# A graph transformer, linear attention and a graph-routed expert layer in one kernel: a reload cut in fifths, a shorter early scatter, two moves, and one-hots transposed on TensorE

## The chip, the cores and the metric

One Trainium2 chip, one of its cores. The metric is device time in microseconds for one execution. Three executions of the kernel before took 7434.32, 7432.77 and 7426.59 us: median 7432.77.

## The reference, cut to what matters

```python
xn = layernorm(x)                                   # x: 6250 nodes x 256
x = x + gnn(xn, edges) + mix(xn)                    # edges: 200,000 pairs src, dst
x = x + ffn(layernorm(x), edges)

def gnn(x, edges):                                  # 6250 x 256 -> 6250 x 256, inner width 128, 8 heads
    e = x @ W_P + b + pos
    for (q, k, v, s, t) in two layers:              # per edge: exp(clip(q[row] . k[col])) per head
        att = exp(clip((e[rows] @ q) * (e[cols] @ k) summed per head, -10, 10))
        e = layernorm(segment_sum(att * (e[cols] @ v), rows) / segment_sum(att, rows) + e) * s + t
    return e @ inv_w + inv_b

def mix(x):                                         # linear attention over all nodes, 8 heads
    q, k, v = elu(rms(x) @ w_q) + 1, elu(rms(x) @ w_k) + 1, rms(x) @ w_v
    h = x + (q @ (k.T @ v)) / (q @ sum(k)) @ w_out + b_out
    return h + rms(h)

def ffn(x, edges):                                  # 4 heads x 4 experts, 131,072 of ffn's own edges
    h = x @ W_gat
    e = leaky_relu(a_src[src] + a_dst[dst]); top = segment_max(e, dst)
    w = exp(e - top[dst])                           # softmax per target node
    agg = segment_sum(w * h[src], dst) / segment_sum(w, dst)
    gate = softmax of the two best of layernorm(agg) over experts
    return sum over 4 experts of gate[e] * (gelu(x @ W1[e] + b1[e]) @ W2[e] + b2[e])
```

## The kernel before, in words

Nodes lie in 50 tiles of 125. Edges are first sorted by the tile of their target; a sorted edge tile holds 128 edges that all point into one node tile. Sums over edges are then matrix products with one-hot matrices: edge by node-in-tile (`hot`), or its transpose (`hot_t`).

The kernel is a row of blocks. Each block ends in a barrier that all engines reach, so a block lasts as long as its longest chain, its DMA waits included. The blocks, in order:

- **place** sorts the graph's 200,000 edges and scatters packed records into a table in HBM. **unpack** (line 531) reads the table back (`lists`), unpacks indices and local node numbers, and stores the local numbers to HBM as rows (`loc_rows`). Its SyncE queue also issues the load of x (5 chunks of 10 tiles, each in two pieces, 1120 and 130 KB) through `also`, ahead of that store, and waits for the store at its end.
- **enter** (line 1771): layer norm, the projection and the first q, k, v, a node tile at a time. TensorE's order for step n is `times_w(n)`, `turn(n+1)`, `project(n-1)`. ScalarE's is `copy_kv(n-1)` (two copies: q, and k with v), then `copy_turned(n+1)`. `times_w(n+1)` waits for `copy_turned(n+1)`. The turned tiles share one PSUM buffer.
- **att1** and **att2** (`attend`, line 705): 417 groups of 4 edge tiles. GpSimd issues 4 indirect gathers of k and v for each group into 4 slots, and takes a slot again when VectorE has weighted it (`weighted`). SyncE loads the group's local numbers, broadcast to all partitions, 4 groups ahead. A second body of work runs in the same steps: in att1 the keys of the linear attention and the sort of the second edge list, in att2 the rest of the linear attention (`Mix`, line 1514), a tile every 8 steps. The second sort keeps its 27 blocks of packed records in SBUF: the first 14 (`SCATTER_FIRST`) in `placed.early`, which lies in the memory of x (the arena), the others in `placed.late`. Mix needs x again: `Mix.sync` issues all 5 chunks ahead of `load_local`'s first load.
- **between** (line 2030): the norm of layer 1, then q, k, v of layer 2, in chunks of 10 tiles. GpSimd clears the sums of each chunk and scatters its share of the 14 early record blocks, 3 indirect DMAs a block, and waits for each block before the next.
- **leave** (line 2128): the norm of layer 2, the output projection, the second layer norm. GpSimd scatters the 13 late blocks. A second unpack follows.
- **max** (`neighbour_max`): maximum over neighbours, beside the expert layer.
- **sum** (`neighbour_sum`, line 2455): 141 steps of 8 edge tiles. `near_hot` compares the broadcast local numbers with the lane number and gives `hot_t`; `fetch` multiplies it by node data; `gather_info`, `sums`, `leaky`, `less`, `exps`, `weigh` make the weights; `high`, `rest_of`, `middle`, `low` split them into three bf16 parts; `one_hot` makes `hot` on VectorE; `add_up` multiplies; `add_sum(0..3)` adds into `acc3`, each waiting for the one before. What an engine does in step n, and in what order, is the list given to `steps`: a pair (lag, piece) runs the piece for k = n + lag. VectorE: info(n), add 0, leaky, add 1, near_hot(n+2), add 2, one_hot(n-2), add 3. GpSimd: sums(n), less(n-1), weigh(n-2), rest_of(n-3), low(n-4). TensorE: add_up(n-5), fetch(n+1).
- **gates** and **answer**: routing weights, weighted sum of the experts' results, output.

Of the kernel before, what the change touches and what calls it, by code (L numbers as in the profile page):

```python
# [8 lines left out]
ALU = mybir.AluOpType  # L9
# [515 lines left out]
def unpack(nc, st, c, g, also=None, loc_type=BF16, sign=1.0):  # L525
# [5 lines left out]
    with ExitStack() as us:  # L531
# [9 lines left out]
        @block.sync  # L541
        def _(sp):
            sp.dma_start(lists[:], g.table.rearrange("(q p l) -> p q l", p=LANES, l=LANES)).then_inc(m["lists_in"], 16)
            if also is not None:
                also(sp)
            sp.wait_ge(m["row_ready"], 1)
            sp.dma_start(g.loc_rows.rearrange("(q p l) -> p q l", p=LANES, l=LANES), row16[:])\
                .then_inc(m["rows_out"], 16)
            sp.wait_ge(m["rows_out"], 16)

# [438 lines left out]

SCATTER_FIRST = 14  # L990

# [520 lines left out]
class Mix:  # L1512
# [39 lines left out]
    def sync(self, sp):  # L1552
        m, ins = self.m, self.ins
        sp.dma_start(self.wq[:], ins["L0_mix_w_qkv"][:, 0:GIN].rearrange("(c p) n -> p c n", p=LANES))\
            .then_inc(m["w_in"], 16)
        sp.dma_start(self.wo[:], ins["L0_mix_w_out"].rearrange("(c p) n -> p c n", p=LANES)).then_inc(m["w_in"], 16)
        sp.dma_start(self.w1[:], ins["L0_mix_w_norm1"].rearrange("(c p) -> p c", p=LANES),
                     allow_slow_non_contiguous=True).then_inc(m["w_in"], 16)
        sp.dma_start(self.b[:], ins["L0_mix_b_out"].rearrange("(a n) -> a n", a=1)).then_inc(m["w_in"], 16)
        load_row(sp, self.w2[:], ins["L0_mix_w_norm2"], m["w_in"])  # L1560
        load_row(sp, self.shift[:], ins["L0_gnn_inv_b"], m["w_in"])
        load_x(sp, ins, self.X, self.x_in)

    def load(self, sp, n):
        pass

# [193 lines left out]

def load_x(sp, ins, X, x_in):

    source = ins["x"].rearrange(TILE_ROWS, p=NODE_TILE)
    for i in range(X.shape[1] // CHUNK):
        a = slice(i * CHUNK, (i + 1) * CHUNK)
        deal(sp, X[:, a], source[:, a], x_in[i])


def enter(nc, c, ins, x_in, X, E, qs, kv, acc, mean, rstd, mean_rstd, mix_rstd, ratio, x_turned):
# [4 lines left out]
    with ExitStack() as st:  # L1774
# [166 lines left out]
        def _(act):  # L1941
# [24 lines left out]
            for n in range(-early, tiles + 1):  # L1966
                if closed(n + early):
                    a = chunk_of(n + early)
                    act.wait_ge(m["var_ready"], (n + early) // CHUNK + 1)
                    act.activation(rstd[:, a], var[:, a], ACT.Sqrt, bias=c.eps5[0:NODE_TILE, 0:1])\  # L1970
                        .then_inc(m["std_ready"], 1)
                if closed(n + early - 1):
                    a = chunk_of(n + early - 1)
                    act.wait_ge(m["ms_ready"], (n + early - 1) // CHUNK + 1)
                    act.activation(ratio[:, a], ratio[:, a], ACT.Sqrt, bias=c.eps6[0:NODE_TILE, :])\
                        .then_inc(m["root_ready"], 1)
                if 0 <= n - 1 < tiles:
                    copy_kv(n - 1, (n - 1) % 2)
                if 0 <= n + 1 < tiles:
                    copy_turned(n + 1, (n + 1) % 2)  # L1980
            act.wait_ge(m["q_copied"], tiles)
# [47 lines left out]

def between(nc, c, ins, acc, E, qs, kv, placed):  # L2030

    tiles = E.shape[1]
    chunks = tiles // CHUNK
    with ExitStack() as st:
# [17 lines left out]
        def _(sp):  # L2052
            normal.sync(sp)
            for i, n in enumerate("qkv"):
                sp.dma_start(w[:, i * D:(i + 1) * D], ins[f"L0_gnn_{n}2"]).then_inc(m["w_in"], 16)
            rows = kv[0:NODES].rearrange("(t p) d -> t p d", p=NODE_TILE)
            for t in range(tiles):
# [398 lines left out]
def neighbour_sum(nc, c, g, src_sb, node_info, gacc, ans):  # L2456

    pairs = WIDE // PAIR
    with ExitStack() as st:
# [3 lines left out]
        def psum(n):  # L2463
            return [st.enter_context(nc.psum_tensor(f"gs_{n}{h}", [LANES, 512], F32)) for h in range(2)]

        node_no = sb("node_no", [LANES, WIDE, NODE_TILE], BF16)
        hot = sb("hot", [LANES, 4, WIDE, NODE_TILE], BF16)
        local = sb("local", [LANES, 4, WIDE * LANES], BF16)
        hot_t = sb("hot_t", [NODE_TILE, 2, WIDE * LANES], BF16)
        info = sb("info", [LANES, 4, WIDE, 2 * FH])  # L2470
# [6 lines left out]
        ps_n, ps_sum = psum("ps_n"), psum("ps_sum")  # L2477
        m = sem_set(nc, st, "gs", ["tiles_in", "cleared", "one_hots", "near_hots", "fetched", "info", "sums", "leaky",
                                   "less", "exps", "weighted", "high", "rest", "middle", "split", "summed", "added",
# [55 lines left out]
        def _(pe):  # L2535
# [7 lines left out]
            def fetch(k, r, j):  # L2543
                pe.wait_ge(m["near_hots"], k + 1)
                wait(pe, m["info"], k - 1)
                for p in range(pairs):
                    t = numbers.of(k * pairs + p)
                    for e in range(PAIR * p, PAIR * (p + 1)):
                        ins = pe.matmul(ps_n[j % 2][:, e * SPLIT * 2 * FH:(e + 1) * SPLIT * 2 * FH],
                                        hot_t[:, j % 2, e * LANES:(e + 1) * LANES],  # L2550
                                        at(node_info, t).rearrange("p n f -> p (n f)"), start=True, stop=True)
                ins.then_inc(m["fetched"], 1)

            def add_up(k, r, j):
# [9 lines left out]
                ins.then_inc(m["summed"], 1)  # L2564
            steps(pe, [(1, load_tiles), (-5, add_up), (1, fetch)])

        @block.scalar
        def _(act):
# [10 lines left out]
            def middle(k, r, j):  # L2579
                act.wait_ge(m["rest"], k + 1)  # L2580
                act.copy(parts[:, k % 4, :, 1, :], rest[:, k % 4]).then_inc(m["middle"], 1)
            steps(act, [(-3, high), (-4, middle), (-1, exps)])

        @block.vector
        def _(dve):
            chain = Chain(dve, m["chain"])
            dve.memset(acc3[:], 0.0)
            chain(dve.tensor_copy(node_no[:], c.node_no[:, 0:1, :].broadcast_to([LANES, WIDE, NODE_TILE])))
            dve.wait_ge(m["tiles_in"], 16)
# [6 lines left out]

            def one_hot(k, r, j):
                wait(dve, m["summed"], (k - 4) + 1)
                dve.tensor_tensor(hot[:, k % 4], node_no[:], g.loc[:, bass.ds(k * WIDE, WIDE)].unsqueeze(2)
                                  .broadcast_to([LANES, WIDE, NODE_TILE]), ALU.is_equal).then_inc(m["one_hots"], 1)  # L2600

            def near_hot(k, r, j):
                dve.wait_ge(m["local_in"][j], (r + 1) * 16)
                wait(dve, m["fetched"], k - 1)
                dve.tensor_scalar(hot_t[:, j % 2, :], local[0:NODE_TILE, j], c.lane_no[0:NODE_TILE, :], None, ALU.is_equal)\
                    .then_inc(m["near_hots"], 1)
# [11 lines left out]
            def add_sum(p):  # L2618
                def add(k, r, j):
# [7 lines left out]
            steps(dve, [(0, gather_info), (-6, add_sum(0)), (-1, leaky), (-6, add_sum(1)), (2, near_hot), (-6, add_sum(2)),  # L2627
                        (-2, one_hot), (-6, add_sum(3)), (-6, load_tiles)])
            dve.wait_ge(m["added"], pairs * total)
# [280 lines left out]
def program(nc, ins, out):  # L2910
    with ExitStack() as ctx:
# [27 lines left out]
        with ExitStack() as gs:  # L2939
# [3 lines left out]
            x_again = gs.enter_context(semaphores(nc, [f"x_again{i}" for i in range(tiles // CHUNK)]))  # L2943
            unpack(nc, gs, c, gnn, lambda sp: load_x(sp, ins, X, x_in), F32, -1.0)
            acc = sb(gs, "acc", [NODE_TILE, tiles, SUMS])
# [5 lines left out]
            with ExitStack() as qs_stack:  # L2951
# [5 lines left out]
                kept.close()  # L2957
                between(nc, c, ins, acc, E, qs, kv, placed)
                attend(nc, c, "att2", gnn, qs, kv, acc, lambda st: Mix(nc, c, st=st, **mix))
# [38 lines left out]
```

## Time and profile before

| | us |
|---|---|
| executions | 7434.32, 7432.77, 7426.59 |
| profiled execution | 7436.28 |
| its span, first to last instruction | 7434.6 |

| engine | busy us | share |
|---|---|---|
| TensorE matmul | 5178.4 | 70% |
| VectorE | 5381.4 | 72% |
| ScalarE | 2567.8 | 35% |
| GpSimd | 5053.4 | 68% |

Stages in the trace, by start, in us from the span's start: unpack 539, enter 575, att1 742, between 2964, att2 3074, leave 5222, second unpack 5393, max 5410, sum 6866, gates and answer 7294. Shares are averages over stages with different limits, so each stage is read by itself. In a row, PE is TensorE's matmul and PEld its weight load, DVE VectorE, ACT ScalarE, POOL GpSimd, SP SyncE; a q behind the name is the engine's queue of DMA issues; L and a number is a line of the kernel, which may be a helper's.

### The profile page before, as it was taken

What the parts mean: (1) busy time and instruction counts of PE and PEld (TensorE: products, weight loads), DVE (VectorE), ACT (ScalarE), POOL (GpSimd) and SP (SyncE); (2) the same over time, 40 slices, a digit from 0 to 9 for tenths busy, and PEclk for the clock granted to TensorE, in tenths of its full rate; (3) what the DMA queues carried; (4) which work ended last, traced back from release to release, by engine and by line L of the source; (5) the groups of instructions that cost most, each with busy time, mean ns of one, the idle gap of its engine ahead of it and who ended that gap; (6) DMA issues with size and microseconds to landing.
All of it is one profiled execution on the core that took longest, in us unless ns stands there. A gap on an engine that the chain in (4) does not pass through costs nothing. (4 is left out here: it accounts for less than half of the span.)

```text
span 7434.6 us, 108730 instructions
## 1 busy us (share of the span) xinstructions
PE 5178.4 (70%) x27327; PEld 4108.7 (55%) x27327; DVE 5381.4 (72%) x15227; ACT 2567.8 (35%) x8277; POOL 5053.4 (68%) x5420
## 2 busy tenths in 40 slices
PE   5985676767777776466666666666679999998440
PEld 3654455556666665256656555555546666665330
DVE  8983676667777776467777777776767777777997
ACT  0002444443344433344444444444322222222330
POOL 1430677777777776577777777777267777776991
PEclk7558788887878777777777888888668888887555
DMA  1013544444444443444444444444323323232437
GB/s 27 4 26 92 138 138 137 139 130 122 124 121 124 124 124 110 112 132 131 131 131 131 131 131 131 131 131 129 106 52 63 60 59 63 59 63 60 121 92 185
DMA packets 510444, 783.73 MB, mean 105 GB/s; under 512 B 121690, under 2 KB 370617, under 8 KB 509837
## 3 DMA queue, kind: packets, MB, share of 16 engines
q0 software_dynamic: 202656, 454.22, 23.2%
q1 hardware_dynamic: 299233, 311.35, 15.5%
q10 hardware_dynamic: 7948, 11.21, 0.6%
q8 instruction: 241, 3.95, 0.2%
q14 instruction: 366, 3.00, 0.1%
HBM read 705.00 MB, written 71.36 MB: 104 GB/s over the span
## 5 line engine op out<-in xcount | busy, mean ns | idle before, releaser
L695 POOL DMA_INDIRECT att_kv_e<-kv,gnn_idx x3336 | 3278.6, 983 | 1238.2 <-issue 984.7
L772 PE MATMUL att_ps_sum<-att_vals,att_hot 128*125 128x136 f32 x6672 | 1290.7, 350 | 1358.1 <-DVE att_vals L826 1356.8
L772 PEld LDWEIGHTS att_ps_sum<-att_vals,att_hot 128*125 128x125 f32 x6672 | 1095.9, 238 | 1588.7 <-DVE att_vals L826 1572.4
L695 POOL DMA_INDIRECT max_rows<-rows,gat_idx x1128 | 1065.6, 945 | 469.5 <-issue 337.4
L807 DVE TENSOR_TENSOR att_prod<-att_ps_q,att_kv_e 128x512 f32<-128x512 f32 x834 | 575.9, 691 | 990.0 <-issue 401.9
L759 PE MATMUL att_ps_q<-qs,att_hot_t 125*128 x6672 | 1182.1, 336 | 104.8 <-DVE att_hot_t L814 104.8
L759 PEld LDWEIGHTS att_ps_q<-qs,att_hot_t 125*128 125x128 f32 x6672 | 1127.8, 254 | 106.1 <-issue 106.1
L790 ACT ACTIVATE att_hot<-node_no,gnn_loc 128x125 f32<-128x125 f32 x3336 | 1044.4, 384 | 22.8 <-PEq L86 22.8
L783 ACT ACTIVATE att_ps_dve<-att_clipped 128x32 f32<-128x32 f32 x834 | 167.7, 201 | 2442.0 <-DVE att_clipped L834 2441.3
L2399 DVE CUSTOM_DVE_ANT_0 max_junk<-max_far,max_ps_b 125x256 bf16<-125x256 bf16 x2256 | 793.3, 416 | 260.2 <-PE max_ps_b L2363 258.7
L842 DVE TENSOR_TENSOR acc<-acc,att_ps_sum 125x136 f32 x1668 | 485.6, 291 | 125.2 <-DVE acc L842 8.2
L820 DVE TENSOR_REDUCE att_dots<-att_prod 128x32 f32<-128x512 f32 x834 | 563.8, 676 | 0.1
L826 DVE TENSOR_TENSOR att_vals<-att_kv_e,att_ps_dve 128x512 f32<-128x512 f32 x834 | 563.6, 676 | 0.0
L795 ACT ACTIVATE att_hot<-att_hot 128x500 f32<-128x500 f32 x834 | 513.9, 616 | 17.4
L2798 PE MATMUL ex_ps_o<-ex_w,ex_hid 128*125 128x256 f32 x1600 | 518.4, 480 | 0.0
L814 DVE TENSOR_SCALAR att_hot_t<-att_local,lane_no 125x512 f32<-125x512 bf16 x834 | 416.1, 499 | 123.6 <-DMA att_local<-gnn_loc_rows 123.6
L2363 PE MATMUL max_ps_b<-max_a_t,pick_head 12*125 12x512 bf16 x1128 | 376.1, 434 | 64.7 <-ACT max_a_t L2372 52.1
L2824 ACT ACTIVATE ex_hid<-ex_ps_h,ex_b 128x250 f32<-128x250 f32 x400 | 165.6, 465 | 726.5 <-PE ex_ps_h L2809 726.4
L2809 PE MATMUL ex_ps_h<-ex_xT,ex_w 128*128 128x250 f32 x1600 | 414.2, 404 | 0.0
L2798 PEld LDWEIGHTS ex_ps_o<-ex_w,ex_hid 128*125 128x125 f32 x1600 | 356.6, 235 | 88.9 <-issue 14.2
L510 POOL DMA_INDIRECT gnn_table<-gnn_records,gnn_dest_sb x120 | 173.9, 1449 | 337.7 <-DVE gnn_records L426 300.5
L2809 PEld LDWEIGHTS ex_ps_h<-ex_xT,ex_w 128*128 128x128 f32 x1600 | 343.4, 215 | 57.8 <-issue 0.4
(450 smaller groups left out, 7501.2 us busy)
## 6 DMA issues: line engine op xcount, KB each, us to landing
att_local<-gnn_loc_rows SPq DMA_DIRECT2D x834, 128.0 KB
att_kv_e<-kv,gnn_idx POOLq DMA_INDIRECT x3336
max_local<-gat_loc_rows SPq DMA_DIRECT2D x282, 128.0 KB
gs_local<-gat_loc_rows SPq DMA_DIRECT2D x141, 256.0 KB, 3.2
outs<-ex_y SPq DMA_DIRECT2D x25, 896.0 KB
max_rows<-rows,gat_idx POOLq DMA_INDIRECT x1128
X<-in_x SPq DMA_DIRECT2D x10, 1120.0 KB
ans_late<-outs SPq DMA_DIRECT2D x11, 896.0 KB
```

What stands on the lines that cost most here:

```text
L695: pool.indirect_dma_start(rows(j, e), None, source, bass.IndirectOffsetOnAxis(ap=g.idx[:, t:t + 1], axis=0))\
L759: ins = pe.matmul(ps_q[j % 2][:, e * D:(e + 1) * D], hot_t[:, j % 2, e * LANES:(e + 1) * LANES], at(qs, t), start=True, stop=True)
L772: ins = pe.matmul(ps_sum[j % 2][0:NODE_TILE, p * 256:p * 256 + SUMS], hot[:, j, PAIR * p + e, :], vals[:, j % 2, PAIR * p + e, :], start=e ...
L790: act.activation(hot[:, j, e, :], c.node_no[:, 0, :], ACT.Abs, bias=g.loc[:, t:t + 1])\
L795: act.activation(hot[:, j], hot[:, j], ACT.Relu, scale=-1.0, bias=1.0).then_inc(m["one_hots"], 1)
L807: dve.tensor_tensor(prod[:].rearrange("p (e d) -> p e d", e=GROUP), ps_q[j % 2][:, :].rearrange("p (e d) -> p e d", e=GROUP), kv_e[:, j, : ...
L820: dve.tensor_reduce(dots_sb[:, j % 2, :], prod[:].rearrange("p (h d) -> p h d", d=HEAD), AX, ALU.add).then_inc(m["dots"], 1)
L826: dve.tensor_tensor(vals[:, j % 2, :, 0:D].rearrange("p e (h d) -> p e h d", d=HEAD), kv_e[:, j, :, D:2 * D].rearrange("p e (h d) -> p e h ...
L842: dve.tensor_tensor(a, a, ps_sum[j % 2][0:NODE_TILE, p * 256:p * 256 + SUMS], ALU.add)\
L2399: ins = dve.tensor_tensor_reduce(out=junk[:, j % 2, 2 * n + i, :], in0=far[:, j % 2, i * 256:(i + 1) * 256], in1=ps_b[n][0:NODE_TILE, i * ...
L2798: ins = pe.matmul(self.ps_o[0:NODE_TILE, 0:GIN], self.hid[:, e % 2, hc, k * NODE_TILE:(k + 1) * NODE_TILE], self.w2[:, e, hc, :], start=hc ...
L2809: ins = pe.matmul(self.ps_h[:, i * TWO:(i + 1) * TWO].rearrange("p (t n) -> p t n", t=2), self.w1[:, e, ch, a:a + LANES], self.xT[:, s % 2 ...
```

## The change

- `unpack` issues the store of `loc_rows`, and waits for it, on ScalarE instead of SyncE. It serves both graphs.
- `SCATTER_FIRST` is 8 instead of 14: 8 record blocks are scattered in between, 19 in leave.
- x is reloaded chunk by chunk: chunk 0 in between, ahead of its k and v stores; chunks 1 to 4 in att2, at steps 40, 120, 200 and 280.
- In enter, ScalarE does `copy_turned(n+1)` ahead of `copy_kv(n-1)`.
- In sum, `one_hot` and its constant are gone. `turn_hots(n-1)`: 8 transposes of `hot_t` on TensorE, behind fetch, into two new PSUM buffers. `copy_hots(n-2)`: one copy of them into `hot` on ScalarE, behind exps. `hot_t` has 4 buffers, which come free on the transposes.

```diff
@@ unpack
-            sp.wait_ge(m["row_ready"], 1)
-            sp.dma_start(g.loc_rows..., row16[:]).then_inc(m["rows_out"], 16)
-            sp.wait_ge(m["rows_out"], 16)
+        @block.scalar
+        def _(act):
+            act.wait_ge(m["row_ready"], 1)
+            act.dma_start(g.loc_rows..., row16[:]).then_inc(m["rows_out"], 16)
+            act.wait_ge(m["rows_out"], 16)
@@
-SCATTER_FIRST = 14
+SCATTER_FIRST = 8
@@ Mix
-        load_x(sp, ins, self.X, self.x_in)                       # in sync
     def load(self, sp, n):
-        pass
+        i, late = divmod(n + MIX_PACE * CHUNK // 2, MIX_PACE * CHUNK)
+        if late == 0 and 0 < i < self.tiles // CHUNK:
+            load_x(sp, self.ins, self.X, self.x_in, i, i + 1)
@@ load_x
-    for i in range(X.shape[1] // CHUNK):
+    for i in range(first, last):
@@ enter, ScalarE
+                if 0 <= n + 1 < tiles:
+                    copy_turned(n + 1, (n + 1) % 2)
                 if 0 <= n - 1 < tiles:
                     copy_kv(n - 1, (n - 1) % 2)
-                if 0 <= n + 1 < tiles:
-                    copy_turned(n + 1, (n + 1) % 2)
@@ between, SyncE, behind the loads of w
+            load_x(sp, ins, X, x_in, 0, 1)
@@ neighbour_sum
-        node_no = sb("node_no", [LANES, WIDE, NODE_TILE], BF16)
-        hot_t = sb("hot_t", [NODE_TILE, 2, WIDE * LANES], BF16)
+        hot_t = sb("hot_t", [NODE_TILE, 4, WIDE * LANES], BF16)
+        ps_hot = [... nc.psum_tensor(f"gs_ps_hot{h}", [LANES, 1024], BF16) for h in range(2)]
+            def turn_hots(k, r, j):                                # TensorE
+                wait(pe, m["one_hots"], k - 1)
+                for e in range(WIDE):
+                    ins = pe.transpose(ps_hot[j % 2][:, e * LANES:e * LANES + NODE_TILE],
+                                       hot_t[:, k % 4, e * LANES:(e + 1) * LANES], c.ident16[0:NODE_TILE, 0:NODE_TILE])
+                ins.then_inc(m["turned"], 1)
-            steps(pe, [(1, load_tiles), (-5, add_up), (1, fetch)])
+            steps(pe, [(1, load_tiles), (-5, add_up), (1, fetch), (-1, turn_hots)])
+            def copy_hots(k, r, j):                                # ScalarE
+                act.wait_ge(m["turned"], k + 1)
+                wait(act, m["summed"], (k - 4) + 1)
+                act.copy(hot[:, k % 4], ps_hot[j % 2][:]....[:, :, 0:NODE_TILE]).then_inc(m["one_hots"], 1)
-            steps(act, [(-3, high), (-4, middle), (-1, exps)])
+            steps(act, [(-3, high), (-4, middle), (-1, exps), (-2, copy_hots)])
-            def one_hot(k, r, j):                                  # VectorE
-                wait(dve, m["summed"], (k - 4) + 1)
-                dve.tensor_tensor(hot[:, k % 4], node_no[:], g.loc[...]..., ALU.is_equal).then_inc(m["one_hots"], 1)
             def near_hot(k, r, j):
-                wait(dve, m["fetched"], k - 1)
+                wait(dve, m["turned"], (k - 4) + 1)
-            steps(dve, [(0, gather_info), (-6, add_sum(0)), (-1, leaky), (-6, add_sum(1)), (2, near_hot), (-6, add_sum(2)),
-                        (-2, one_hot), (-6, add_sum(3)), (-6, load_tiles)])
+                        (-6, add_sum(3)), (-6, load_tiles)])
```

## Rows read from the trace of the kernel before

**Rows 1.** Timeline, unpack's end: start, length, engine, line, operation, [idle before, releaser].
```profile
539.87 23.62 SPq L649 DMA_DIRECT2D X<-in_x  x10
563.53 0.49 SPq L547 DMA_DIRECT2D gnn_loc_rows<-gnn_row  x1
575.20 5.76 POOL L1834 MEMSET acc<- 125x6800 f32 x1 [39.56 <-POOLq L86]
```

**Rows 2.** Timeline of one tile of enter.
```profile
729.58 0.81 PE L1929 MATMUL enter_ps_p<-enter_w,enter_ET 128*125 128x384 f32 x2
...
730.85 0.39 ACT L1957 COPY enter_xT<-enter_ps_t 128x250 f32<-128x250 f32 x1
...
731.29 0.71 PE L1921 MATMUL enter_ps_e<-enter_xT,enter_wp 128*128 128x125 f32 x4 [0.90 <-ACT enter_xT L1957]
```

**Rows 3.** Waits in enter: engine, line, releaser, us in total, times, longest.
```profile
PE enter_ps_e L1921 <- ACT enter_xT L1957: 44.2, 50, 0.9
```

**Rows 4.** Timeline of the end of enter: last stores, first issue of att1.
```profile
736.64 2.35 SPq L649 DMA_DIRECT2D kv<-enter_kv_sb  x4
...
741.92 0.23 SPq L738 DMA_DIRECT2D att_tile_of<-gnn_pair_tile  x1
```

**Rows 5.** Timeline of the end of between and the start of att2.
```profile
3035.86 19.82 SPq L649 DMA_DIRECT2D kv<-between_kv_sb  x29
...
3073.68 0.22 SPq L738 DMA_DIRECT2D att_tile_of<-gnn_pair_tile  x1
...
3076.49 37.66 SPq L649 DMA_DIRECT2D X<-in_x  x10
...
3123.46 0.88 DVE L814 TENSOR_SCALAR att_hot_t<-att_local,lane_no 125x512 f32<-125x512 bf16 x2 [84.24 <-DMA att_local<-gnn_loc_rows]
...
3130.56 0.94 POOL L695 DMA_INDIRECT att_kv_e<-kv,gnn_idx  x1 [36.45 <-DVE att_vals L826]
```

**Rows 6.** Tile `gat_table`, scatters: ns min/median/max, first to last start, form.
```profile
L1010 POOL DMA_INDIRECT gat_table<-X,placed_dest x42: 952/999/2094, 2980.9 to 3066.4; - x42
L1010 POOL DMA_INDIRECT gat_table<-placed_late,placed_dest x39: 952/958/1947, 5223.6 to 5310.5; - x39
```

**Rows 7.** Windows, sum stage: stretch, us, busy us by engine, clock, DMA share, GB/s.
```profile
6866.00:7294.00 428.00, 180.28 (x2256) 165.46 (x2256) 415.77 (x1133) 123.81 (x423) 408.71 (x705) 0.50 0.34 100
```

**Rows 8.** Timeline of VectorE in one step of sum.
```profile
7103.53 1.19 DVE L2599 TENSOR_TENSOR gs_hot<-gs_node_no,gat_loc 128x1000 bf16<-128x1000 bf16 x1
...
7106.44 1.19 DVE L2599 TENSOR_TENSOR gs_hot<-gs_node_no,gat_loc 128x1000 bf16<-128x1000 bf16 x1
...
7107.55 0.20 DVE L2623 TENSOR_TENSOR gs_acc<-gs_acc,gs_ps_sum 125x60 f32 x1
```

**Rows 9.** Timeline of VectorE in sum's last steps: one add behind another.
```profile
7284.42 0.22 DVE L2623 TENSOR_TENSOR gs_acc<-gs_acc,gs_ps_sum 125x60 f32 x1 [0.21 <-DVE gs_acc L2623]
```

**Rows 10.** Timeline of GpSimd in one step of sum.
```profile
7104.79 0.41 POOL L2508 TENSOR_TENSOR gs_vals<-src_sb,gs_vals 128x128 f32<-128x128 f32 x1
...
7106.46 1.28 POOL L2530 TENSOR_TENSOR gs_e_sb<-gs_e_sb,gs_info 128x32 f32<-128x32 f32 x1
```

**Rows 11.** Tile `gs_e_sb`, columns as in rows 6.
```profile
L2610 DVE SCALAR_TENSOR_TENSOR gs_e_sb<-gs_e_sb x141: 174/511/518, 6873.5 to 7276.4; 128x32 f32<-128x32 f32 x141
L2530 POOL TENSOR_TENSOR gs_e_sb<-gs_e_sb,gs_info x141: 244/1275/1281, 6874.1 to 7277.3; 128x32 f32<-128x32 f32 x141
```

**Rows 12.** Tile `gs_hot_t`, columns as in rows 6.
```profile
L2605 DVE TENSOR_SCALAR gs_hot_t<-gs_local,lane_no x141: 472/639/765, 6870.8 to 7268.7; 125x1024 bf16<-125x1024 bf16 x141
```

**Rows 13.** Timeline of TensorE in one step of sum.
```profile
7106.16 1.06 PE L2560 MATMUL gs_ps_sum<-gs_parts,gs_hot 128*125 128x60 bf16 x8 [1.64 <-POOL gs_parts L2520]
...
7107.04 0.39 PE L2549 MATMUL gs_ps_n<-node_info,gs_hot_t 125*128 x8
```

**Rows 14.** Timeline of TensorE in max: four transposes.
```profile
6000.35 0.39 PE L2354 MATMUL max_ps_a<-ident,max_rows 128*12 128x128 bf16 x4
```

**Rows 15.** Lines, a ScalarE copy: busy us, mean ns, idle before.
```profile
L2372 ACT COPY max_a_t<-max_ps_a 12x512 bf16<-12x512 bf16 x282 | 161.9, 574 | 371.9 <-PE max_ps_a L2354 371.9
```

More of the change, by code:

```diff
@@ L545, in _ @@
                 also(sp)
-            sp.wait_ge(m["row_ready"], 1)
-            sp.dma_start(g.loc_rows.rearrange("(q p l) -> p q l", p=LANES, l=LANES), row16[:])\
+        @block.scalar
+        def _(act):
+            act.wait_ge(m["row_ready"], 1)
+            act.dma_start(g.loc_rows.rearrange("(q p l) -> p q l", p=LANES, l=LANES), row16[:])\
                 .then_inc(m["rows_out"], 16)
-            sp.wait_ge(m["rows_out"], 16)
+            act.wait_ge(m["rows_out"], 16)
         @block.tensor
@@ L1758, with load_x @@
 CHUNK = 10
-def load_x(sp, ins, X, x_in):
+def load_x(sp, ins, X, x_in, first, last):
     source = ins["x"].rearrange(TILE_ROWS, p=NODE_TILE)
-    for i in range(X.shape[1] // CHUNK):
+    for i in range(first, last):
         a = slice(i * CHUNK, (i + 1) * CHUNK)
@@ L2027, in scalar, with between @@
             .then_inc(m["root_ready"], 1)
-def between(nc, c, ins, acc, E, qs, kv, placed):
+def between(nc, c, ins, acc, E, qs, kv, placed, X, x_in):
     tiles = E.shape[1]
@@ L2477, in neighbour_sum @@
         ps_n, ps_sum = psum("ps_n"), psum("ps_sum")
-        m = sem_set(nc, st, "gs", ["tiles_in", "cleared", "one_hots", "near_hots", "fetched", "info", "sums", "leaky",
+        ps_hot = [st.enter_context(nc.psum_tensor(f"gs_ps_hot{h}", [LANES, 1024], BF16)) for h in range(2)]
+        m = sem_set(nc, st, "gs", ["tiles_in", "cleared", "turned", "one_hots", "near_hots", "fetched", "info", "sums", "leaky",
                                    "less", "exps", "weighted", "high", "rest", "middle", "split", "summed", "added",
@@ L2549, in fetch @@
                         ins = pe.matmul(ps_n[j % 2][:, e * SPLIT * 2 * FH:(e + 1) * SPLIT * 2 * FH],
-                                        hot_t[:, j % 2, e * LANES:(e + 1) * LANES],
+                                        hot_t[:, k % 4, e * LANES:(e + 1) * LANES],
                                         at(node_info, t).rearrange("p n f -> p (n f)"), start=True, stop=True)
                 ins.then_inc(m["fetched"], 1)
+            def turn_hots(k, r, j):
[4 more added lines that the diff above has]
+                ins.then_inc(m["turned"], 1)
             def add_up(k, r, j):
@@ L2581, in middle @@
                 act.copy(parts[:, k % 4, :, 1, :], rest[:, k % 4]).then_inc(m["middle"], 1)
-            steps(act, [(-3, high), (-4, middle), (-1, exps)])
+            def copy_hots(k, r, j):
+                act.wait_ge(m["turned"], k + 1)
+                wait(act, m["summed"], (k - 4) + 1)
+                act.copy(hot[:, k % 4], ps_hot[j % 2][:].rearrange("p (e n) -> p e n", e=WIDE)[:, :, 0:NODE_TILE])\
+                    .then_inc(m["one_hots"], 1)
+            steps(act, [(-3, high), (-4, middle), (-1, exps), (-2, copy_hots)])
         @block.vector
@@ L2586, in _ @@
             chain = Chain(dve, m["chain"])
-            dve.memset(acc3[:], 0.0)
-            chain(dve.tensor_copy(node_no[:], c.node_no[:, 0:1, :].broadcast_to([LANES, WIDE, NODE_TILE])))
+            chain(dve.memset(acc3[:], 0.0))
             dve.wait_ge(m["tiles_in"], 16)
@@ L2595, in gather_info @@
                                   .rearrange("p (e n f) -> p e f n", e=WIDE, n=SPLIT), AX, ALU.add).then_inc(m["info"], 1)
-            def one_hot(k, r, j):
-                wait(dve, m["summed"], (k - 4) + 1)
-                dve.tensor_tensor(hot[:, k % 4], node_no[:], g.loc[:, bass.ds(k * WIDE, WIDE)].unsqueeze(2)
-                                  .broadcast_to([LANES, WIDE, NODE_TILE]), ALU.is_equal).then_inc(m["one_hots"], 1)
             def near_hot(k, r, j):
                 dve.wait_ge(m["local_in"][j], (r + 1) * 16)
-                wait(dve, m["fetched"], k - 1)
-                dve.tensor_scalar(hot_t[:, j % 2, :], local[0:NODE_TILE, j], c.lane_no[0:NODE_TILE, :], None, ALU.is_equal)\
+                wait(dve, m["turned"], (k - 4) + 1)
+                dve.tensor_scalar(hot_t[:, k % 4, :], local[0:NODE_TILE, j], c.lane_no[0:NODE_TILE, :], None, ALU.is_equal)\
                     .then_inc(m["near_hots"], 1)
@@ L2943, in program @@
             x_again = gs.enter_context(semaphores(nc, [f"x_again{i}" for i in range(tiles // CHUNK)]))
-            unpack(nc, gs, c, gnn, lambda sp: load_x(sp, ins, X, x_in), F32, -1.0)
+            unpack(nc, gs, c, gnn, lambda sp: load_x(sp, ins, X, x_in, 0, tiles // CHUNK), F32, -1.0)
             acc = sb(gs, "acc", [NODE_TILE, tiles, SUMS])
@@ L2957, in program @@
                 kept.close()
-                between(nc, c, ins, acc, E, qs, kv, placed)
+                between(nc, c, ins, acc, E, qs, kv, placed, X, x_again)
                 attend(nc, c, "att2", gnn, qs, kv, acc, lambda st: Mix(nc, c, st=st, **mix))
```

## The prediction, made before the change was run

> **What bounds the kernel now.** I read the windows by stage first, then the waits of each stage that the change touches, then the timeline where a wait ends last. A barrier stands between stages, so what a stage loses is lost for good.
>
> In unpack the reader is to see SyncE: its issue of x ends at 539.87 + 23.62 = 563.49, the store behind it goes out at 563.53, and enter starts only at 575.20 [rows 1]. In enter TensorE stands still for 0.90 us in each tile until the turned tile is copied [rows 2], 44.2 us over 50 tiles [rows 3]. Between ends with the scatters: the last starts at 3066.4 [rows 6], the k and v stores are issued by 3035.86 + 19.82 = 3055.68, and att2 starts at 3073.68 [rows 5]. In att2 GpSimd's gathers set the pace, but it stands for 36.45 us once, since the first local numbers land behind all of x: VectorE waits 84.24 us for them [rows 5]. In sum VectorE is busy 415.77 of 428 us and GpSimd 408.71; TensorE runs at a granted clock of 0.50, its 1.2 GHz level [rows 7]. One step takes 7106.44 - 7103.53 = 2.91 us, and `one_hot` has 7107.55 - 7106.44 = 1.11 of it [rows 8]. While it runs, GpSimd's `less` takes 1.275 us instead of 0.244 [rows 10, 11]: both engines wait for one thing.
>
> **The change part by part.** The sum goes against the profiled execution, 7436.28 us; the median of the runs is 3.5 below it.
>
> *Unpack's store.* It leaves ScalarE as soon as VectorE has the rows, and SyncE's end is then the end of the issue of x. From the end of the last issue to the first of the next block enter took 741.92 - 738.99 = 2.93 us, with landing [rows 4]; so enter can start near 563.49 + 2.9 = 566.4, 8.8 us earlier. The store is 0.46 MB beside 6.4 MB of x, whose issue may take 1.7 us longer (23.62 x 0.46 / 6.4). Enter's first weights now move while x still lands. Bounds: 0 (the store lands as late as now) to -10. I take -7, nearer to the SyncE row. The other unpack has no load of x in front: 0. The row says that the store waits behind x in its queue. The Trainium skill (DMA: Bandwidth & Descriptors, Issuing engines are not separate DMA queues) says that transfers from all issuing engines run on the same 16 DMA engines and interleave; it speaks against a gain beyond the issue. By it alone this term would be the 0.49 us of issue, by the rows it is 7.
>
> *Enter's copies.* ScalarE copies the next turned tile while `project` (0.81 us) runs: the copy takes 0.39 [rows 2], and `turn` stands ahead of `project`. So the 0.90 goes: 50 x 0.90 = 45. Queued behind the moved copy are q, k and v of the tile before; only `project` of the next step waits for them, a whole `times_w` and `turn` later. Late next is VectorE: a step of 2.0 us leaves little beside its chain of statistics every tenth tile. Bounds -20 (half is lost there or to stores that now come every 2 us) to -45. I take -40, near the row.
>
> *Between.* 42 scatters took 2980.9 to 3066.4, 2.04 us each [rows 6]. 24 fit in 49 us, and the last chunk has 6 instead of 9. Then the stores end last: 3055.68 + 2.93 = 3058.6, against 3073.68: -15. Chunk 0 of x, 1.25 MB, goes out ahead of the first store, where the queue is idle while VectorE norms its first chunk: 0; without that cover it would delay the stores by 7.5 us, a fifth of 37.66 [rows 5]. Bounds -8 to -18.
>
> *Leave* gets 18 more scatters: 39 took 86.9 us [rows 6], so 57 take 127 and end near 5351, over 40 us ahead of the next block at 5393: 0; at worst +5 by crowding the stores.
>
> *att2's start.* The local loads go out at 3076.49 instead of 37.7 us later, so the first slot comes free near 3130.56 - 37.7 = 3092.9. GpSimd has gathers to issue until 3130.56 - 36.45 = 3094.1 [rows 5]. All 36.45 go. In return four chunks run during the gathers, each with 7.5 us of queue time ahead of the local loads of four groups. A group lasts 5.15 us (417 in 2148 us), and loads run four groups, 20 us, ahead: hidden, but I leave 2.5 for it. Without the cover it is 4 x 7.5 = 30. Bounds -6 to -36.5; I take -34, near the cover.
>
> *Sum.* VectorE loses 1.11 of 2.91 us. But `add 2` and `add 3` now stand side by side, and each add waits for the one before: 0.22 + 0.21 = 0.43 us from one to the next [rows 9], where one now takes 0.20 [rows 8] with other work between: +0.23, or +0.3 with the issue. That is 2.1. GpSimd: from `weigh` at 7104.79 to `less` at 7106.46 are 1.67 us [rows 10], with an undisturbed `less` 1.9. TensorE: `add_up` and `fetch` from 7106.16 to 7107.43, 1.27 [rows 13], and 8 transposes. Max did four in 0.39 us [rows 14]; at the 1.2 GHz level eight are 0.8 to 0.9 (125 columns each): 2.1 to 2.2 at that clock, less if it rises. ScalarE: 123.81 / 141 = 0.88 a step [rows 7] and one copy of 1000 columns. No row has it; 512 columns took 0.574 [rows 15], so it lies between 0.6 and 1.12: at most 2.0. All four engines then need 1.9 to 2.2, and I take a step of 2.2, a tenth over VectorE's: 0.71 x 138 steps in the steady part = 98. Bounds: a step of 1.9 gives -139, one of 2.9 gives 0. Two waits are new. `turn_hots` waits for the copy two steps back, with `add_up` queued behind it; `add_up` waits for `copy_hots`, which ran two steps ahead. Neither is last as long as ScalarE keeps up.
>
> Sum: 7 + 40 + 15 + 34 + 98 = 194. 7436.28 - 194 - 3.5 = **7239 us**.
>
> **Rivals.** *The shared port (20%).* `less` shows that a VectorE instruction and one of GpSimd exclude each other [rows 10, 11]. `hot_t` and `leaky` stretch too, 0.472 to 0.639 and 0.174 to 0.511 [rows 11, 12]. If they exclude all of GpSimd's work, a step is 1.91 + 0.47 + 0.17 = 2.55: 0.36 x 138 = 50 instead of 98, 7287 us. Against it: GpSimd's 1.67 us were measured with both of them beside it. The Trainium skill (SBUF — State Buffer, Who interferes with whom) has such a rule: VectorE with two inputs in SBUF, or in its two-port modes, and GpSimd lock one port pair for a whole instruction. By that rule the trace agrees for `one_hot`.
>
> *x in the way of the local loads (10%).* Each chunk stops the gathers for its 7.5 us; 30 of the 36 come back: 7267. For it: they stood 36 us for that in the trace; against it: that was at a start, with no group ahead.
>
> *TensorE in series, slower (4%).* `add_up` waits for the last of GpSimd's pieces, `fetch` stands behind it, the transposes behind that. If the two steps of lag that part these are eaten up, a step is 1.9 + 1.27 + 0.86 = 4.03 us: 1.12 x 138 = +155, with the other terms, -96, and the 3.5: 7492. It decides from 2.91 + 96 / 138 = 3.6 us a step. For it: TensorE waits 1.64 us for that piece in each step [rows 13]; against: with the same lags this costs the step nothing today.
>
> *More than forecast (10%).* A step of 1.95, enter 44, between 18: 7 + 44 + 18 + 36 + 132 = 237, 7196.
>
> **How the numbers follow.** The forecast has 56%, with a range of its own of 7205 to 7275. The range 7185 to 7310 takes in the port, the queue and most of the better case. Leaving out 4% for the slow rival and 1% for terms that just cancel: faster 0.95, same 0.01, slower 0.04 (0.2%, 15 us, is what a measurement of this kernel can tell from none).
>
> **What would show it.** Enter within 3 us of unpack's last issue of x; no wait of TensorE for the turned tile and about 2.0 to 2.1 us a tile; att2 starting right behind the last k and v stores; no gap of GpSimd at att2's start, and none at steps 40, 120, 200 and 280; in sum steps of 2.2 us with `less` near 0.25 to 0.45. I am wrong if ScalarE's copy takes over 1.2 us, if TensorE's transposes hold up `fetch`, or if VectorE waits in enter.

## The result, and the profile after

The changed kernel takes 7250.86 us (median of 4, 7240.77 to 7260.62) against 7431.77 beside it: ratio 0.9757, 95% interval [0.974, 0.9774]. Forecast was 7239. The profiled execution is the slowest of the four, 7260.62. Stages are read from their first instructions. The change in means compares the traces of all runs, those of the experiments below included, that have the old or the changed code in that stage; in brackets stands how many have the changed code.

| stage | before | after | change in means | forecast |
|---|---|---|---|---|
| unpack's end | 35.8 | 30.2 | -7.1 (10 runs) | -7 |
| enter | 166.7 | 117.4 | -48.8 (9) | -40 |
| att1 | 2223.5 | 2216.5 | -1.2 (11) | 0 |
| between | 108.3 | 93.1 | -14.7 (9) | -15 |
| att2 | 2150.0 | 2128.7 | -29.5 (7) | -34 |
| leave, second unpack | 186.1 | 186.1 | +1.0 (10) | 0 |
| max | 1456.5 | 1456.7 | +0.5 (11) | 0 |
| sum | 427.9 | 348.9 | -81.7 (6) | -98 |
| gates, answer | 140.4 | 140.8 | +0.3 (11) | 0 |

The means add up to -181; the medians differ by 180.9. att1 and att2 vary by some 10 us from run to run, mostly in the sum of their gathers' own durations (1593.5 to 1602.8 us in att2), so one pair of traces can't size a few us there.

The timeline at unpack's end (start, length, engine, line, operation, [idle before]) answers to [rows 1]: x's issue ends at 569.62, and enter starts 1.1 us behind it instead of 11.7.

```profile
540.98 28.64 SPq L652 DMA_DIRECT2D X<-in_x  x10
...
551.73 0.42 ACTq L550 DMA_DIRECT2D gnn_loc_rows<-gnn_row  x1
...
570.73 5.76 POOL L1838 MEMSET acc<- 125x6800 f32 x1 [33.98 <-POOLq L86]
```

One tile of enter, as [rows 2]: the copy now runs beside `project`, and the next product follows at once. One tile takes 661.22 - 659.40 = 1.82 us.

```profile
659.40 0.81 PE L1933 MATMUL enter_ps_p<-enter_w,enter_ET 128*125 128x384 f32 x2
...
659.60 0.37 ACT L1961 COPY enter_xT<-enter_ps_t 128x250 f32<-128x250 f32 x1 [0.63 <-PE enter_ps_t L1916]
...
660.04 0.68 PE L1925 MATMUL enter_ps_e<-enter_xT,enter_wp 128*128 128x125 f32 x4
...
661.22 0.81 PE L1933 MATMUL enter_ps_p<-enter_w,enter_ET 128*125 128x384 f32 x2
```

Of the 44.2 us of waits in [rows 3] 2.3 are left:

```profile
PE enter_ps_e L1925 <- ACT enter_xT L1961: 2.3, 6, 0.5
```

Between's end, as [rows 5]: att2's first issue stands 2.9 us behind the last store's (2979.96 + 14.89 = 2994.85).

```profile
2979.96 14.89 SPq L652 DMA_DIRECT2D kv<-between_kv_sb  x22
2997.72 0.22 SPq L741 DMA_DIRECT2D att_tile_of<-gnn_pair_tile  x1
```

The scatters, as [rows 6]: the last early one starts at 2987.2, before the issue of those stores ends; the 57 late ones take 130 us of leave and end well ahead of the next block.

```profile
L1013 POOL DMA_INDIRECT gat_table<-placed_late,placed_dest x57: 952/959/2032, 5126.4 to 5256.6; - x57
L1013 POOL DMA_INDIRECT gat_table<-X,placed_dest x24: 954/1004/1820, 2920.3 to 2987.2; - x24
```

Waits of GpSimd in att2 (us, times, longest): the 36.45 of [rows 5] is gone, the longest is 2.3.

```profile
POOL att_kv_e L698 <- DVE att_vals L829: 18.7, 44, 2.3
```

Sum by windows, as [rows 7], and by the tiles of [rows 11, 12]: VectorE has fallen from 97% to 73% of the stage, TensorE has risen from 42% to 86%, still at a granted clock of 0.51, its 1.2 GHz level. `less` is back at 0.252.

```profile
6769.00:7110.00 341.00, 292.56 (x3382) 259.58 (x3383) 249.60 (x981) 219.92 (x564) 275.85 (x705) 0.51 0.42 126
```

```profile
L2535 POOL TENSOR_TENSOR gs_e_sb<-gs_e_sb,gs_info x141: 246/252/255, 6776.5 to 7102.2; 128x32 f32<-128x32 f32 x141
```

```profile
L2616 DVE TENSOR_SCALAR gs_hot_t<-gs_local,lane_no x141: 478/742/746, 6773.1 to 7096.3; 125x1024 bf16<-125x1024 bf16 x141
```

The steps are not equal: from one `info` to the next they take mostly 2.04 and 2.67 us in turn, 2.32 on average over the stage. The timeline of VectorE shows the two adds standing one behind the other, and in every second step 0.52 us in which VectorE waits for nothing that the profile names:

```profile
6942.03 0.20 DVE L2634 TENSOR_TENSOR gs_acc<-gs_acc,gs_ps_sum 125x60 f32 x1
6942.44 0.22 DVE L2634 TENSOR_TENSOR gs_acc<-gs_acc,gs_ps_sum 125x60 f32 x1 [0.21 <-DVE gs_acc L2634]
6943.18 0.36 DVE L2610 TENSOR_REDUCE gs_info<-gs_ps_n 128x64 f32<-128x192 f32 x1 [0.52 <-issue]
...
6945.22 0.35 DVE L2610 TENSOR_REDUCE gs_info<-gs_ps_n 128x64 f32<-128x192 f32 x1
```

What fills the 0.52 is not counted as busy. It is found under the tile that holds the node-tile numbers: `load_tiles` reads 8 of them into registers in every second step, 0.597 us on VectorE's own queue.

```profile
L669 DVEq TENSOR_LOAD <-gs_tile_of x1: 597/597/597, 6942.5 to 6942.5; - x1
```

Before, the same read took as long, but it started at 7103.8, inside the `one_hot` of 7103.53 to 7104.72 [rows 8]:

```profile
L666 DVEq TENSOR_LOAD <-gs_tile_of x2: 594/594/594, 7103.8 to 7109.7; - x2
```

So `one_hot` had been the cover of a read, and went.

### The profile page after: what moved, and what is told of

Same layout as the page of the kernel before. It is cut to its first block and busy times, and to the rows that moved or that the text cites. A ratio compares the mean times of both kernels' runs of the same rounds, so it can differ in the third digit from the quotient of the medians.

```text
span 7258.9 us, 111120 instructions
## 1 busy us (share of the span) xinstructions
PE 5273.1 (73%) x28455; PEld 4201.6 (58%) x28455; DVE 5222.9 (72%) x15085; ACT 2669.1 (37%) x8418; POOL 4921.1 (68%) x5420
## 3 DMA queue, kind: packets, MB, share of 16 engines
q0 software_dynamic: 202656, 454.22, 23.6%
## 5 line engine op out<-in xcount | busy, mean ns | idle before, releaser
L775 PE MATMUL att_ps_sum<-att_vals,att_hot 128*125 128x136 f32 x6672 | 1306.6, 354 | 1364.5 <-DVE att_vals L829 1363.5
```

Source lines behind the costliest of these rows:

```text
L775: ins = pe.matmul(ps_sum[j % 2][0:NODE_TILE, p * 256:p * 256 + SUMS], hot[:, j, PAIR * p + e, :], vals[:, j % 2, PAIR * p + e, :], start=e ...
```

## The experiments

**A cover for the read.** Two pieces of VectorE's list change places:

```diff
-(-6, add_sum(1)), (2, near_hot), (-6, add_sum(2)), (-6, add_sum(3)), (-6, load_tiles)
+(-6, add_sum(1)), (-6, add_sum(2)), (2, near_hot), (-6, add_sum(3)), (-6, load_tiles)
```

> The changed kernel with one pair swapped in VectorE's list for sum: add 2 now ahead of near_hot, so that near_hot (0.74 us) stands between add 2 and add 3. Theory (uncovered register load): steps of the changed kernel alternate between 2.04 and 2.67 us because every second step VectorE's sequencer reads 8 node-tile numbers into registers (about 0.6 us) with nothing left running on the engine; before, one_hot ran during that read. With near_hot running during it, all steps are 2.04 to 2.1: mean 2.1 instead of 2.32, sum 31 us shorter, median about 7220 (7212 to 7228). Rival A (TensorE or GpSimd set the step, the alternation is theirs): nothing changes, 7245 to 7255. Rival B (the wait of one add for another is what counts): a wait goes between add 2 and add 3 and one comes between add 1 and add 2: nothing changes.

7241.28 us, ratio 0.9741 [0.9727, 0.9754], 10 below the changed kernel, whose interval it overlaps. The stage shows the gain: sum takes 331.7, -14 against the mean of 346.1 (343.1 to 349.0 in six runs). The long steps fell from 2.67 to 2.31, the short ones stayed (2.07), so neither rival holds; but the size is half of what was expected. The read begins at 6991.4, once add 2 (6990.97 to 6991.19) is done, for which add 3 waits ahead of it. It ends at 6992.0, behind add 3, and `info` starts only at 6992.14 (VectorE's timeline, and the read's row):

```profile
6990.97 0.22 DVE L2634 TENSOR_TENSOR gs_acc<-gs_acc,gs_ps_sum 125x60 f32 x1 [0.21 <-DVE gs_acc L2634]
6991.11 0.76 DVE L2616 TENSOR_SCALAR gs_hot_t<-gs_local,lane_no 125x1024 bf16<-125x1024 bf16 x1
6991.79 0.20 DVE L2634 TENSOR_TENSOR gs_acc<-gs_acc,gs_ps_sum 125x60 f32 x1
6992.14 0.36 DVE L2610 TENSOR_REDUCE gs_info<-gs_ps_n 128x64 f32<-128x192 f32 x1
```

```profile
L669 DVEq TENSOR_LOAD <-gs_tile_of x1: 599/599/599, 6991.4 to 6991.4; - x1
```

**The read right behind its cover.** `add_sum(2), near_hot, load_tiles, add_sum(3)`.

> The changed kernel with VectorE's list for sum in the order add 1, add 2, near_hot, load_tiles, add 3. The run with near_hot ahead of add 3 alone brought the long steps from 2.67 to 2.31 us and left the short ones at 2.07. Theory (part of the register read still shows): add 3 waits for add 2, so the read began only after that wait and its last 0.24 us came out behind add 3; put straight behind near_hot it lies wholly beside it. All steps 2.07 to 2.1, sum 315 to 318 us, 15 us less than with near_hot alone: about 7226. Rival (the remaining alternation is TensorE's own register read, which it makes every second step too): steps stay 2.07 and 2.31, sum about 332, 7241.

7243.22 us (0.9738 [0.9724, 0.9751]), no different from the run above; sum 329.0, 2.7 less instead of 15. The long steps are mostly 2.23 and the short ones 2.10, so neither the theory nor the rival holds. VectorE's timeline has a long step (6988.31 to 6990.55) and a short one behind it:

```profile
6988.31 0.34 DVE L2610 TENSOR_REDUCE gs_info<-gs_ps_n 128x64 f32<-128x192 f32 x1
...
6989.59 0.77 DVE L2616 TENSOR_SCALAR gs_hot_t<-gs_local,lane_no 125x1024 bf16<-125x1024 bf16 x1
6990.41 0.22 DVE L2634 TENSOR_TENSOR gs_acc<-gs_acc,gs_ps_sum 125x60 f32 x1
6990.55 0.35 DVE L2610 TENSOR_REDUCE gs_info<-gs_ps_n 128x64 f32<-128x192 f32 x1
...
6991.83 0.77 DVE L2616 TENSOR_SCALAR gs_hot_t<-gs_local,lane_no 125x1024 bf16<-125x1024 bf16 x1
6992.52 0.20 DVE L2634 TENSOR_TENSOR gs_acc<-gs_acc,gs_ps_sum 125x60 f32 x1
6992.64 0.34 DVE L2610 TENSOR_REDUCE gs_info<-gs_ps_n 128x64 f32<-128x192 f32 x1
```

The read now starts with `near_hot`:

```profile
L669 DVEq TENSOR_LOAD <-gs_tile_of x1: 599/599/599, 6989.6 to 6989.6; - x1
```

It ends at 6990.19, and add 3 behind it starts at 6990.41: 0.82 us after `near_hot`, where it is 0.69 without a read (6991.83 to 6992.52). So 0.13 us of the read still show in every second step. TensorE is close behind VectorE: over the stage its waits for GpSimd's last piece were 39.8 us in the changed kernel, 16.0 in the first repair, and here

```profile
PE gs_ps_sum L2572 <- POOL gs_parts L2525: 4.6, 14, 1.0
```

(waits in sum: us, times, longest). With `add_up`, `fetch` and the transposes back to back at a granted clock of 0.50, its 1.2 GHz level, it needs 2.07 us a step (in the changed kernel `add_up` starts at 6993.08 and again at 6995.15, with no gap between).

**The read twice as often.** Four numbers in each step:

```diff
-            numbers = TileNumbers(nc, dve, tile_of, g)
+            numbers = TileNumbers(nc, dve, tile_of, g, 4)
```

> The changed kernel with VectorE's register read in sum made twice as often: 4 tile numbers in every step instead of 8 in every second. Theory (an uncovered read lengthens the step that it stands in): every step is long, by 0.63 us if a read of 4 costs what a read of 8 does (2.67 us), by 0.3 if it goes with the numbers read (2.35): sum 349 to 390 us, and no step of 2.04 left. Rival (the alternation of 2.04 and 2.67 belongs to the two PSUM buffers or to TensorE's read, and VectorE's read is beside the point): the alternation stays as it is, sum 343 to 349.

7270.94 us beside 7445.66: 0.9766 [0.975, 0.9782]; sum 349.2. A read of 4 takes 0.345 us, `info` waits 0.27 in nearly every step, and the turn of 2.04 and 2.67 is gone: steps are 2.39, some 2.12. The wait goes where the read goes, which settles it. The read's row, and VectorE's timeline:

```profile
L669 DVEq TENSOR_LOAD <-gs_tile_of x141: 342/345/355, 6777.8 to 7116.5; - x141
```

```profile
6991.43 0.48 DVE L2616 TENSOR_SCALAR gs_hot_t<-gs_local,lane_no 125x1024 bf16<-125x1024 bf16 x1
...
6992.73 0.36 DVE L2610 TENSOR_REDUCE gs_info<-gs_ps_n 128x64 f32<-128x192 f32 x1 [0.27 <-issue]
...
6993.56 0.74 DVE L2616 TENSOR_SCALAR gs_hot_t<-gs_local,lane_no 125x1024 bf16<-125x1024 bf16 x1
...
6995.12 0.36 DVE L2610 TENSOR_REDUCE gs_info<-gs_ps_n 128x64 f32<-128x192 f32 x1 [0.27 <-issue]
```

The steps of 2.12 (6990.61 to 6992.73) are those in which `near_hot` takes 0.48 instead of 0.74. All 101 long ones here run across the start of GpSimd's `rest_of`; 29 of the 35 short ones stand beside `weigh`. That the port is behind this is inferred from the overlap; no run tests it.

**The cover taken away before.** In the kernel before, `one_hot` goes ahead of add 2.

> The kernel before with one pair swapped in VectorE's list for sum: one_hot ahead of add 2, so that add 2, add 3 and the register load stand at the end without a long instruction over them, as in the changed kernel. Theory (uncovered register load): every second step pays 0.5 to 0.6 us for the read, and each step 0.2 for add 3 behind add 2, less what GpSimd catches up while VectorE stands: 0.3 to 0.5 us a step on average, +40 to +70 us, 7470 to 7500. The steps alternate. Rival A (the load costs nothing anywhere): +28 us at most, from the wait between the adds, and equal steps. Rival B (GpSimd and the shared port set the step of 2.91): within 10 us of before.

7542.32 us, +111: more than any theory said. Steps of 3.45 and 4.08 mostly take turns, 0.63 apart as in the changed kernel, so the read shows here too. But the short steps are 0.54 longer as well, against 0.2 expected. In most steps `one_hot` now lies across GpSimd's `low`, and both stretch: `one_hot` from 1.186 us (its median before) to 1.484, `low` from 0.491 to 1.445 (the first and the second row are of this run, the third of the kernel before):

```profile
L2599 DVE TENSOR_TENSOR gs_hot<-gs_node_no,gat_loc x141: 1185/1484/1493, 6879.7 to 7395.0; 128x1000 bf16<-128x1000 bf16 x141
L2520 POOL TENSOR_TENSOR gs_parts<-gs_rest,gs_parts x141: 487/1445/1451, 6886.1 to 7397.5; 128x160 bf16<-128x160 f32 x141
L2520 POOL TENSOR_TENSOR gs_parts<-gs_rest,gs_parts x141: 485/491/675, 6881.7 to 7282.9; 128x160 bf16<-128x160 f32 x141
```

VectorE's starts account for the 0.54: from `one_hot` to the next start 0.30 us more, from add 2 to add 3 0.29, from `near_hot` 0.10, and from `leaky`, which no longer stretches, 0.14 less.

**Sum as before, all else changed.**

> The changed kernel with sum as it was before (one_hot on VectorE, no transposes); all else as changed. Theory (stages add up, since a barrier parts them): sum 428 us instead of 343 to 349, +79 to +85, about 7332; every stage ahead as in the changed kernel. Rival (part of sum's gain comes from the stages ahead, by the state of the DMA queues or of TensorE's clock at its start): sum 420 or less.

7327.19 us, 0.9852 [0.9836, 0.9867], +76; sum 427.6 us. The stages add up, as expected.

**The old order of enter's copies.**

```diff
-                if 0 <= n + 1 < tiles:
-                    copy_turned(n + 1, (n + 1) % 2)
                 if 0 <= n - 1 < tiles:
                     copy_kv(n - 1, (n - 1) % 2)
+                if 0 <= n + 1 < tiles:
+                    copy_turned(n + 1, (n + 1) % 2)
```

> The changed kernel with ScalarE's copies in enter in the old order. Theory (the order of the copies alone is worth the whole change of enter): the step is 2.91 us again instead of 1.82 and enter takes 166 us instead of 117: +49, about 7300. Rival (part of enter's gain is not from the order, but from x's landing earlier against enter's start, or from the store on ScalarE's queue): enter 160 or less, +40 or less.

7303.77 us, 0.9822 [0.9805, 0.984], +53; enter 169.3 us, 52.0 more than the mean of 117.3 and 3.2 more than in the two runs of the kernel before (166.1). The order alone carries the term, and TensorE's 50 waits are back:

```profile
PE enter_ps_e L1925 <- ACT enter_xT L1961: 44.4, 50, 1.1
```

**The store on SyncE again.**

> The changed kernel with unpack's store of the local numbers on SyncE again. Theory: unpack's end takes 35.8 us again instead of 28.9 to 30.2: +6 to +7 us there, and nothing elsewhere; in the median 7250 to 7260. Rival (the shared DMA engines finish x and the store at the same time in either order, so enter only waits for x later): unpack's end +6, enter as much shorter, no change in their sum.

7267.52 us, 0.977 [0.9754, 0.9786]: not clear of the changed kernel's interval. By the trace unpack's end is 38.5 us (+9.7 against the mean of 28.8) and enter 114.2 (-3.1): +6.6 net. The rival has a third of it. The 3 us stand at enter's start: there the changed kernel's VectorE waits 2.90 us for enter's weights, and with the store on SyncE it doesn't wait. The DMA engines are busy until then, most likely with what is left of x: their share is 0.69 at 575 to 580 us and 0.02 at 580 to 585. The first matmul comes 12.8 us after enter's start in the changed kernel, 9.8 here and in the kernel before. The changed kernel's row:

```profile
582.25 0.29 DVE L1900 TENSOR_TENSOR enter_bias<-enter_bias,enter_pos 125x128 f32<-125x128 f32 x1 [2.90 <-DMA enter_w<-in_L_gnn_v]
```

**x at once; then the scatters 14 and 13 too.** `load_x` for all chunks in `sync`, none in `load` and in between; then `SCATTER_FIRST = 14`.

> The changed kernel with x again reloaded whole at the start of att2, ahead of the first local numbers, and no chunk in between; the scatters stay split 8 and 19. Theory (stall moved to four small ones): GpSimd's stall of about 36 us at the start of att2 comes back, four gaps of about 2 us each in it go: +29 us against the changed kernel, about 7280; between stays at 93 us. Rival (the chunks among the gathers slow all gathers, which is why att2 gained 21 and not 29): the gathers of att2 take 1597 us in sum again instead of 1604, and the difference is 21, about 7272.

> The changed kernel with x reloaded whole at att2's start and the scatters split 14 and 13 again. Against the kernel with only the reload undone (7285 us, between 92.8 us, leave with the second unpack 186.7): theory (6 blocks fewer are worth the 15 us that between lost): between 108, leave the same: +15, about 7300. Rival (chunk 0 of x in between is free and the scatters are too; between lost its time to something else): between 93.

7284.95 us (0.98 [0.9785, 0.9815]), +34, and 7305.75 (0.9819 [0.9804, 0.9834]), 21 more. In the first the stall is back, longest 36.3, with between at 92.8 and att2 at 2151.8:

```profile
POOL att_kv_e L698 <- DVE att_vals L829: 49.1, 43, 36.3
```

The rival that the chunks slow all gathers fell: these take 1595.6 us in sum here and 1593.5 to 1602.8 in runs with chunks. In the second, between is 108.5, att2 2154.5, leave 188.0: the scatters are worth the 15 us.

**The chunks from ScalarE's queue.**

```diff
     def scalar(self, act, n):
+        i, late = divmod(n + MIX_PACE * CHUNK // 2, MIX_PACE * CHUNK)
+        if late == 0 and 0 < i < self.tiles // CHUNK:
+            load_x(act, self.ins, self.X, self.x_in, i, i + 1)
```

> The changed kernel with chunks 1 to 4 of x issued by ScalarE instead of SyncE at the same steps of att2. Theory (shared DMA engines): VectorE's wait of 8 to 9 us at each chunk and GpSimd's gap of about 2 us stay, since the gathers' own rows come late while all engines carry x: within 5 us of the changed kernel, 7246 to 7256. Rival (order in SyncE's queue): the local numbers wait only because they stand behind x in one queue; with x elsewhere the four waits and gaps vanish, 7 us less, about 7243. A second rival: ScalarE's issue (1.4 us each time) holds up its copies and the gaps grow.

7250.72 us, 0.9756 [0.9741, 0.9771]: no difference in the whole. In the stage the longest gap falls from 2.3 to 1.0, and GpSimd's idle time (the waits below, without the one ahead of its first gather) is 508.5 instead of 511.8 to 514.9. So the queue decides 3 to 6 us of GpSimd's idle time; the stage itself, 2119.3 us, lies within what the seven other runs with chunks have (2118.4 to 2128.7). VectorE's longest wait ahead of its first product falls from 9.2 to 5.2: the waits neither stay nor vanish, and both theory and rival are half right.

```profile
POOL att_kv_e L698 <- issue: 490.2, 1609, 0.3
POOL att_kv_e L698 <- DVE att_vals L829: 18.3, 58, 1.0
```

**Both repairs together.**

> The changed kernel with both small repairs: VectorE's order add 1, add 2, near_hot, load_tiles, add 3 in sum, and chunks 1 to 4 of x issued by ScalarE in att2. Theory (both add up): sum 329 us instead of about 346, and GpSimd's idle time in att2, without its wait ahead of the first gather, 508 to 509 us instead of 512 to 515: 17 + 5 = 22 below the changed kernel, about 7229. Rival (the queue that x goes through decides nothing in the whole, as the median of that run alone, 7250.7, would have it): 17 less, about 7234. Rival (the sum's gain is lost in the stage behind it): 7250.

7226.75 us (5 runs), ratio 0.9722 [0.9708, 0.9736], 24 below the changed kernel and clear of its interval; sum 327.6, idle time 508.3. Of the 24 the trace shows 18.5 in sum (against the mean of 346.1) and none in att2, which takes 2123.5 us beside a mean of 2122.6 with the chunks on SyncE. The rest is not told apart.

## Why the prediction was right, and where not

*Unpack: -7.1, as forecast, by luck in its size.* The two parts were off and cancelled: enter starts 1.1 us behind the last issue and not 2.9, and the issue of x took 25.6 to 28.6 us instead of 23.6 and 24.3 in two runs of the old order. With the store on SyncE again it took 27.8 as well, so the store is not shown to lengthen it. The Trainium skill (DMA: Bandwidth & Descriptors, Issuing engines are not separate DMA queues) says that another issuer saves issue time alone; by it 0.49 us would have been saved. The 7 disagree: what went is the wait for that store at the end of SyncE's queue. The prediction says that enter's first weights then move while x lands, and gives that no price: it is the wait of 2.90 us at enter's start, so some 3 of the 7 are lost again one stage later (that x is what delays the weights is inferred).

*Enter: -48.8, beyond the bound of 45.* The failing step is "the 0.90 goes", and the deduction from it. From `project`'s start to the next product are 0.64 us now (659.40 to 660.04); before, they were 1.71 (729.58 to 731.29 [rows 2]). So 1.07 went: the pipeline that runs on saves 0.81 - 0.64 = 0.17 of `project`'s row besides the idle time. A whole step fell from 2.91 us to 1.82. Fifty of these 1.09, less 0.5 in every tenth tile for VectorE, are 52, which is what the old order costs; the 3 us of the weights leave 49. The clock also rose sooner, and what that is worth is not told apart. The first matmul came at 583.53 (585.00 before), and the level rises to 2.4 GHz within the window below (us, busy us by engine, granted clock, DMA share, GB/s). In the changed kernel TensorE had by then no gap, 5.00 of 5 us; the kernel before reached it two windows later, with 4.10 of 5 us busy in each:

```profile
590.00:595.00 5.00, 5.00 (x23) 4.03 (x22) 2.08 (x8) 1.82 (x6) 0.00 (x0) 0.63 0.18 53
```

```profile
595.00:600.00 5.00, 4.10 (x15) 2.95 (x15) 1.19 (x4) 0.81 (x3) 0.00 (x0) 0.50 0.22 66
600.00:605.00 5.00, 4.10 (x19) 2.42 (x17) 1.93 (x7) 0.81 (x3) 0.00 (x0) 0.80 0.21 65
```

VectorE's tenth tile costs 0.5 us, as feared, but only that.

*Between: -14.7, by the stores that were named as next.* The 24 scatters took 67 us (2920.3 to 2987.2) and not 49, since GpSimd waits 49 us for VectorE's chunks among them; the issue of the stores ends 8 us behind the last one's start, so they are still hidden. *Leave: the 57 scatters took 130 us against 127, hidden.*

*att2: -29.5 against -34, in bounds.* (Of the 84.24 us that the prediction calls VectorE's wait for the local numbers, 34 lie in between; 50 are of att2, from 3073.68 to 3123.46.) The stall went whole; the four chunks cost more than the 2.5 us left for them. Each makes VectorE wait 8 to 9 us and GpSimd about 2, as the timelines of SyncE and of VectorE have the first one:

```profile
3178.38 1.37 SPq L652 DMA_DIRECT2D X<-in_x  x2
```

```profile
3188.32 0.69 DVE L810 TENSOR_TENSOR att_prod<-att_ps_q,att_kv_e 128x512 f32<-128x512 f32 x1 [8.13 <-issue]
```

The rival by which 30 of the 36 come back is wrong by a factor of four to five: 6 to 7 us come back, and the slots absorb the rest of each wait.

*Sum: -81.7 against -98.* The failing step is VectorE's sum of 2.1 us a step. It counted busy rows, and left out the register read, which had no row among them; the short steps came at 2.04. With most of the read covered the mean step is 2.18, and sum 99 less; that the forecast of 2.2 meets it is partly chance, since its tenth of margin stood for no named cost. ScalarE's copy took 0.974 (between 0.6 and 1.12, as bounded) and the transposes 1.00 (0.8 to 0.9 taken; the four in max ran at a granted clock of 1.00, those in sum at 0.51, which the prediction did not set apart). The port's rival is wrong as a whole: `less` and `leaky` no longer stretch. What is left is `near_hot`, which stretches more than before (0.742 us, 0.639 before), and `rest_of` (0.676, 0.491 before). TensorE in series did not come: its two steps of lag held.

Against the forecast's sum enter came out 9 us better, att2 5 and sum 16 worse: 12 in all, which is the distance of the two times. So the total is nearer than its terms, because enter's surplus hides more than half of what sum fell short.

## What to carry to other kernels

Before a long instruction is taken out, list what its engine's queue does under it: register reads, waits and issues have no busy time and come to light once the cover goes. Put such a read behind the longest instruction, ahead of anything that waits, and count what follows it too: 0.69 us of cover left 0.13 of a 0.6 us read to be seen, since the next instruction started 0.22 us after the read's end; `one_hot`, with 1.11 us, had hidden it whole. And where a wait on TensorE's path goes, expect more than the idle time shown, since the pipeline then runs through.

## What the runs showed of the hardware beyond that

A read of 8 numbers into registers takes 0.597 us, one of 4 takes 0.345. The Trainium skill (DMA: Bandwidth & Descriptors, Latency and other measured facts) gives a floor of some 600 ns for a `tensor_load`; the read of 8 agrees, the read of 4 lies below it. `near_hot`, with one tile as input, takes 0.48 or 0.74 us, the latter where it runs across the start of GpSimd's `rest_of`.
